# Spreading the feed's stages over its nine steps, with other shares and index loads in the tail

## The chip, the cores and the metric

One core of a Trainium2 chip runs the whole program. The metric is the device time of one execution in microseconds; lower is better. The engines are TensorE (PE, with PEld for its weight loads), VectorE (DVE), ScalarE (ACT), GpSimd (POOL) and SyncE (SP), which here issues the plain DMAs. The indirect DMAs are issued by POOL.

## What is computed

Two batches of 4096 tokens of width 256 go through a sparse attention with 16 heads of width 16, a residual sum with a layer norm, a feed part, and a second residual sum with a layer norm.

```python
scores = einsum('bhqd,bhkd->bhqk', q, k) * scale
sparsity = scores.max(axis=-1) - scores.mean(axis=-1)
_, top_idx = top_k(sparsity, U)                      # U = 307 queries of each head
out_sel = softmax(q_sel @ k.T * scale) @ v           # for the chosen queries alone
out = zeros_like(q).at[bi, hi, top_idx].set(out_sel)
x = layernorm(x + out @ Wo + bo)
xr = mu_r * x + (1 - mu_r) * x_prev ; xk = mu_k * x + (1 - mu_k) * x_prev
r = sigmoid(xr @ W_r.T) ; k = xk @ W_k.T
x = layernorm(x + r * (square(relu(k)) @ W_v.T))
```

## The kernel before

Python function `schedule()` writes one list, the plan, of tokens such as `("main", p)` or `("f2", b, t, part, bank, late)`. Every engine walks the same list and issues its own share of each token, in the order of the list. An engine is in order: what it waits for holds up everything behind it.

**The main phase** has 2048 slots, 64 for each of the 32 (batch, head) pairs. A slot is one `main` token: PE makes four 128x512 products (two into CP at L592, two into DP at L596), ACT takes the absolute value of the CP half into AB (L858), and DVE adds AB and the DP half and takes the row maximum (JK, L1014). There are two DP halves and three AB buffers. So PE can be about one slot ahead of DVE, and then waits for DVE to read a DP half (the wait on SPr in the rows).

**What rides on the slots.** After `main` a slot carries one step of the selection (`sel`, which finds the 307 queries of a group of heads), and one step of the attention over chosen queries (`att`), or, where `att` yields `None`, one step of the background (`back`). In the slots of an attention with a selection the slot behind a `cnt` or similar token, and that slot itself, carry neither (`hold`), unless bank "P" is spare. The heads are in seven groups of 8, 5, 3, 5, 5, 3 and 3.

**Attention.** For a head `hl` and a block of keys `kc` (0 to 31) `st` makes scores on PE (L688), exponentials on ACT (E, L896), and the low part of E as the difference to its bf16 high part (EL). EL is computed by POOL (L1411) for share "G" and by DVE (L1163) for share "D". `pv` follows six steps later with two products into PV (L703, L704). There are ten E buffers. At the end of a head come `fin` (ACT L903), `otr` (PE and four short DVE operations, L1170 to L1176) and `put` (POOL: L1420 and three indirect DMAs to AO, L1424). `gath` is three indirect DMAs on POOL (L1384), `arr` seven short POOL operations behind their landing.

**The feed** works through 32 tiles of 128 tokens for each batch. Tile t takes part in iterations k = t to t+9: f0 loads (SP), f1 transposes, f2 product with Wo, sum (DVE L1197) and statistics (`stats`: L1184, L1186, then `rstd` on POOL, L1430 to L1435), f3 normalises, f4 transposes, f5 mixes (POOL L1475 to L1480 in batch 0, DVE L1222 in batch 1), f6 and f6k products (tanh on ACT L934, relu on ACT L942, square on POOL L1490 in batch 0), f7 product and gating (DVE L1234, then a sum on POOL L1498 or DVE L1238), f8 statistics, f9 normalises (POOL L1511 or DVE L1251) and stores (SP L1637). `feed(0, False)` is background of the main phase. `feed(1, True)` runs alone at the end (`late`), with the f3, f5, f9 work on DVE.

**Banks.** `bank()` takes the spare PSUM banks in turn and skips the one in `state["open"]`. `attend` starts only when no bank is open. In the main phase the feed and the selection share two banks, B and P; `claim` makes PE wait until the last reader of a bank is through.

**The tail** is what follows the 2048 slots: the selection of the last group of three heads (group 6) side by side with the rest of group 5's attention, then group 6's indices, gathers and attention, then `feed(1, True)`. Background steps are taken in the tail only when no search is on.

Of the kernel before, what the change touches and what calls it, by code (L numbers as in the profile page):

```python
# [54 lines left out]
def schedule():  # L55
# [64 lines left out]
    def select(g):  # L120
# [39 lines left out]
        for h in range(n):  # L160
            yield [("idx", g, h, bank())]
        yield [("ixdma", g)]

    def prelude(g):

        n = GROUPS[g][2] if tail[0] else 1
        gaps = 0 if tail[0] else 1
        yield [("ka", 0), ("qgzero",)] if g == 0 else []
        yield [("gath", g, 0)]
        for _ in range(5 * gaps):  # L170
            yield []
        for h in range(n):
            yield [("arr", g, h)] + ([("gath", g, h + 1)] if h + 1 < n else [])
        for _ in range(4 * gaps):
            yield []
        ahead[g] = n

    def attend(g):
# [6 lines left out]
        for i in range(total + PVLAG):  # L185
            step = []
            hl, kc = divmod(i, NT)
            if i < total:
                if kc == 0:
                    step.append(("qt", g, hl, "C0"))  # L190
                    if HEAD0[g] + hl + 1 < NB * H:
                        step.append(("ka", HEAD0[g] + hl + 1))
                if kc == 10 and ahead[g] <= hl + 1 < n:
                    step.append(("gath", g, hl + 1))
                if kc == 18 and ahead[g] <= hl + 1 < n:
                    step.append(("arr", g, hl + 1))
                step.append(("st", g, hl, kc, bank(), "D" if tail[0] and kc % 2 and not state["search"] else "G"))
            j = i - PVLAG
# [3 lines left out]
            if j >= 0 and j % NT == NT - 1:  # L202
                yield [("fin", g, j // NT)]
                yield [("otr", g, j // NT, bank()), ("put", g, j // NT)]
                yield []

    def feed(b, late):
        for k in range(NT + 9):
            step = []
            for n in (9, 8, 7, 6, 5, 4, 1, 0, 3, 2):  # L210
                t = k - n
                if not 0 <= t < NT:
                    continue
                if n in (2, 6, 7):
                    for f in ("f6", "f6k") if n == 6 else ("f%d" % n,):
                        bk = state["open"] = bank()
                        for part in range(2):
                            yield step + [(f, b, t, part, bk, late)]
                            step = []
                        state["open"] = None  # L220
                elif n in (1, 4):
                    step.append(("f%d" % n, b, t, bank(), late))
                else:
                    step.append(("f%d" % n, b, t, late))
                if n == 0:
                    yield step
                    step = []
            if step:
                yield step

# [87 lines left out]
def attention_rwkv(nc, x, Wq, bq, Wk, bk, Wv, bv, Wo, bo, W_r, W_k, W_v, mu_r, mu_k, out):  # L318
    ctx = ExitStack()
    with ctx:  # L320
# [115 lines left out]
        l_w, l_z, l_m, l_i, l_q = (sem(n) for n in ("l_w", "l_z", "l_m", "l_i", "l_q"))  # L436
        l_g = [sem(f"l_g{i}") for i in range(4)]
        l_s, l_k, l_o, l_a = ([sem(f"{n}{i}") for i in range(2)] for n in ("l_s", "l_k", "l_o", "l_a"))
        l_x = [sem(f"l_x{i}") for i in range(4)]
# [515 lines left out]
        def _(dve):  # L955
# [233 lines left out]
            def f2(b, t, part, bank, late):  # L1189
# [6 lines left out]
                dve.wait_ge(f_yp, k + 1)  # L1196
                dve.tensor_tensor(fh[j], BANK[bank][:, 0:D], fx[k % 3], ALU.add).then_inc(f_y, 1)  # L1197
                dve.wait_ge(f_y, k + 1)
                stats(fh[j], j, j, f_s1, k + 1)

# [45 lines left out]
            def f9(b, t, late):  # L1246
                if late:
# [7 lines left out]
                          digit=digit, cut=cut, need=need_, rank1=rank1, rank2=rank2, slots=slots, ob=ob, oa=oa, idx=idx,  # L1255
                          st=st, otr=otr, f2=f2, f3=f3, f5=f5, f7=f7, f8=f8, f9=f9)
            for stage, *args in plan:
# [4 lines left out]
        def _(pool):  # L1262
# [110 lines left out]
            def gath(g, h):  # L1373
# [3 lines left out]
                if h == 0:  # L1377
                    pool.wait_ge(l_i, 64 * (g + 1))
                    pool.wait_ge(l_m, 32 * HEAD0[g + 1])
                if hx >= 8:  # L1380
                    pool.wait_ge(q_pool, arranged[hx - 8])
# [64 lines left out]

            def f2(b, t, part, bank, late):
                if part == 0:
                    return
                k = NT * b + t  # L1450
                after(pool, f_x1, k - 1)
                pool.wait_ge(f_s1, k + 1)
                rstd(k % 2, late).then_inc(f_r1, 1)
# [52 lines left out]
            def f9(b, t, late):  # L1506
                if not late:
# [5 lines left out]
            stages = dict(vones=vones, qzero=qzero, split=split, slots=slots, ob=ob, qgzero=qgzero, gath=gath, arr=arrange,  # L1513
                          st=st, put=put, f1=f1, f2=f2, f3=f3, f5=f5, f6k=f6k, f7=f7, f8=f8, f9=f9)
            setup()
# [5 lines left out]
        def _(sp):  # L1521
# [83 lines left out]

            def ixdma(g):
                n = GROUPS[g][2]
                sp.wait_ge(sel_ix, HEAD0[g + 1])
                sp.dma_start(IDX[g, 0:n, 0:16 * A_COLS].rearrange("h (a b) -> a h b", b=16), idw[:, 0:n, :]).then_inc(l_i, 16)
                sp.wait_ge(l_i, 64 * g + 16)  # L1610
                for c, (a0, w) in enumerate(CH):
                    sp.dma_start(idxs[g][0:w, 0:n, c], IDX[g, 0:n, a0:a0 + w].rearrange("h s -> s h")).then_inc(l_i, 16)

# [56 lines left out]
```

## Time and profile before

| | us |
|---|---|
| median of 3 runs (3490.24 to 3497.87) | 3496.7 |
| the profiled execution, whole | 3497.08 |
| its span in the profile | 3495.3 |
| busy: PE, DVE, ACT, POOL | 3113.3, 2940.5, 2878.4, 1491.0 |

The profiled execution is 1.8 us longer than its span; the rest of the text works inside the span. Stretches by the trace: the main phase ends at about 3156 us, the tail's attention and selection last until about 3330 us, and the late feed fills the rest. The feed of batch 0 lies in two stretches of the main phase, about 1990 to 2260 us and 2530 to 2790 us, with the attention of group 3 between them.

### The profile page before, as it was taken

Reading aid. Unit: us, or ns where it says so; the run is one execution under the profiler, and the core shown is the slowest. Engines: PE = TensorE matmul, PEld = TensorE weight load, DVE = VectorE, ACT = ScalarE, POOL = GpSimd, SP = SyncE. Lnnn points to the kernel's source line nnn. Section 1 sums busy time; section 2 is a strip of 40 time slices with the busy share of each in tenths; the row PEclk is TensorE's granted clock in tenths of the full one; section 3 lists DMA queues with packets and bytes.
Section 4 is the critical chain, followed back from the end, with each engine's and each line's share of the span. In section 5 each row is a group of like instructions: output and inputs, shape, how many; then the busy total and the mean of one; then the engine's idle time right before and its main releaser. Section 6 shows DMA issues by size and latency. Waiting matters only on the chain.

```text
span 3495.3 us, 58965 instructions
## 1 busy us (share of the span) xinstructions
PE 3113.3 (89%) x15985; PEld 1442.4 (41%) x15985; DVE 2940.5 (84%) x5954; ACT 2878.4 (82%) x6445; POOL 1491.0 (43%) x2634
## 2 busy tenths in 40 slices
PE   5999999998899998998999888899988898897588
PEld 3334333343244433433444444544444443344366
DVE  2889988899978888888898888888887888886478
ACT  3889888889779999899899877699976699894455
POOL 2210022100136643453556455675555653457754
PEclk8999999999989999999999999999999999997899
DMA  6432232316122241241111241121141222013022
GB/s 183 147 81 36 61 85 76 82 36 15 25 38 38 38 33 27 37 33 31 23 38 29 43 48 42 42 44 36 31 38 42 40 32 31 14 20 15 14 77 69
DMA packets 262295, 163.64 MB, mean 47 GB/s; under 512 B 167563, under 2 KB 241483, under 8 KB 257867
## 3 DMA queue, kind: packets, MB, share of 16 engines
q1 hardware_dynamic: 255819, 158.50, 24.8%
q0 software_dynamic: 6144, 1.37, 0.5%
q8 instruction: 128, 2.10, 0.3%
q14 instruction: 204, 1.67, 0.2%
HBM read 111.86 MB, written 47.86 MB: 46 GB/s over the span
## 4 chain that ended last, share of the span: by engine, by line
PE 32%; ACT 26%; issue 19%; DVE 19%; POOL 2%; DMA 1%; SPq 0%; DVEq 0%; ACTq 0%; POOLq 0%
ACT AB L858 19%; DVE JK L1014 11%; PE CP L592 10%; PE DP L596 9%; ACT E L896 4%; ACT msk L879 2%; PE PV L703 2%; PE PV L704 2%; PE BP L688 2%; DVE SPr L1014 1%; PE PV L540 1%; DVE fst L1184 1%; PE BP L726 1%; PE BP L540 1%; DVE VF L1222 1%
## 5 line engine op out<-in xcount | busy, mean ns | idle before, releaser
L1014 DVE CUSTOM_DVE_ANT_0 JK<-DP,AB 128x1024 bf16<-128x1024 f32 x2048 | 2469.0, 1222 | 384.7 <-DVE SPr L1014 137.7
L858 ACT ACTIVATE AB<-CP 128x512 f32<-128x512 f32 x4096 | 2227.3, 598 | 306.8 <-PE CP L592 253.6
L592 PE MATMUL CP<-KS,QS 128*128 128x512 f16 x4096 | 1425.3, 389 | 96.3 <-ACT AB L858 20.5
L596 PE MATMUL DP<-KS,QS 128*128 128x512 f16 x4096 | 1241.9, 385 | 70.4 <-DVE SPr L1014 63.7
L1411 POOL TENSOR_TENSOR SCR<-E 128x307 f16<-128x307 f32 x968 | 672.5, 706 | 590.7 <-ACT E L896 581.8
L592 PEld LDWEIGHTS CP<-KS,QS 128*128 128x128 f16 x4096 | 393.8, 97 | 883.7 <-ACT AB L858 762.3
L596 PEld LDWEIGHTS DP<-KS,QS 128*128 128x128 f16 x4096 | 361.6, 98 | 402.9 <-DVE SPr L1014 187.3
L896 ACT ACTIVATE E<-BP 128x307 f32<-128x307 f32 x883 | 384.5, 436 | 55.1 <-PE BP L688 53.7
L1266 POOL TENSOR_SCALAR SCR<-SCR 128x48 f16<-128x48 f16 (+2 forms) x122 | 49.6, 406 | 571.7 <-DVE SCR L982 321.6
L688 PE MATMUL BP<-QT,KA 128*128 128x307 f16 x883 | 263.1, 298 | 20.9 <-ACT QT L888 19.1
L703 PE MATMUL PV<-E,XT 128*128 128x307 bf16 x512 | 161.4, 316 | 34.2 <-POOL SCR L1411 34.0
L1014 DVE DVE_READ_ACCUMULATOR2_ANT SPr<- 128x1 f32 x2048 | 168.9, 82 | 0.0
L704 PE MATMUL PV<-SCR,XT 128*128 128x307 f16 x512 | 157.6, 308 | 0.0
L703 PE MATMUL PV<-E,VF 128*128 128x307 bf16 x512 | 153.9, 301 | 0.0
L704 PE MATMUL PV<-SCR,VF 128*128 128x307 f16 x512 | 149.7, 292 | 0.0
L688 PEld LDWEIGHTS BP<-QT,KA 128*128 128x128 f16 x883 | 87.0, 98 | 147.3 <-issue 24.2
L1384 POOL DMA_INDIRECT SCR<-QN,idxs x96 | 99.6, 1037 | 77.2 <-issue 70.4
L1424 POOL DMA_INDIRECT AO<-OG,idxs x96 | 100.8, 1050 | 34.1 <-issue 16.9
L896 ACT ACTIVATE E<-DP 128x307 f32<-128x307 f32 x115 | 47.4, 427 | 48.3 <-PE DP L688 48.1
L1430 POOL TENSOR_SCALAR frs<-fmv 128x1 f32<-128x1 f32 x128 | 29.1, 227 | 132.3 <-DVE fmv L1186 129.6
L703 PEld LDWEIGHTS PV<-E,XT 128*128 128x128 f16 x512 | 52.1, 102 | 80.4 <-POOL SCR L1411 32.7
L1431 POOL TENSOR_TENSOR frs<-frs,halfc 128x1 f32<-128x1 f32 x128 | 78.3, 612 | 10.7
(381 smaller groups left out, 2984.5 us busy)
## 6 DMA issues: line engine op xcount, KB each, us to landing
KS<-KTC SPq DMA_DIRECT2D x256, 128.0 KB, 5.0
QS<-QSC SPq DMA_DIRECT2D x512, 64.0 KB
KA<-KTC SPq DMA_DIRECT2D x128, 128.0 KB, 3.8
QN<-SCR SPq DMA_DIRECT2D x16, 544.0 KB, 3.4
SCR<-in_L_attn_x SPq DMA_DIRECT2D x16, 512.0 KB, 6.8
KTC<-SCR SPq DMA_DIRECT2D x32, 256.0 KB, 2.2
QSC<-SCR SPq DMA_DIRECT2D x32, 256.0 KB, 2.3
AO<-E SPq DMA_DIRECT2D x2, 4096.0 KB, 21.9
```

Source lines behind the costliest of these rows:

```text
L592: pe.matmul(o, qs, ks[j][:, 1, :], start=True, stop=True).then_inc(sc_c, 1)
L596: r = pe.matmul(o[:, 512 * j:512 * j + 512], qs, ks[j][:, 0, :], start=True, stop=True)
L688: pe.matmul(o[:, 0:U], KA[hx % 2][:, 128 * kc:128 * kc + 128], QT[hx % 2][:, 0:U], start=True, stop=True).then_inc(s_pe, 1)
L703: pe.matmul(PV[:, 0:U], v, EH[a % NE], start=kc == 0, stop=False)
L704: pe.matmul(PV[:, 0:U], v, EL[a % NE], start=False, stop=kc == NT - 1).then_inc(pv_pe, 1)
L858: act.activation(AB[p % 3][:, 512 * j:512 * j + 512], BANK["C%d" % j], ACT.Abs).then_inc(ab_full, 1)
L896: act.activation(E[a % NE][:], BANK[bank][:, 0:U], ACT.Exp, scale=2 * SCALE / (WS * WS)).then_inc(ex_act, 1)
L1014: dve.tensor_tensor_reduce(out=JK[p % 2][:], in0=BANK["D%d" % u], in1=AB[p % 3][:], scale=1.0, scalar=-3.0e38, op0=ALU.add, op1=ALU.max, a ...
L1384: pool.indirect_dma_start(out=QG[0:w, 3 * (hx % 8) + c, :], out_offset=None, in_=QNr[b], in_offset=bass.IndirectOffsetOnAxis(ap=ixf[0:w, k ...
L1411: pool.tensor_tensor(EL[a % NE], E[a % NE][:], EH[a % NE], ALU.subtract).then_inc(el_g, 1)
L1424: pool.indirect_dma_start(out=AOr[b], out_offset=bass.IndirectOffsetOnAxis(ap=ixf[0:w, k:k + 1], axis=0), in_=OG[i][0:w, c, :], in_offset= ...
L1431: i = pool.tensor_tensor(r[:, 0:1], r[:, 0:1], halfc[:], ALU.pow)
```

## The change

1. `feed` gives every iteration in steps of its own by a table, `products`. An entry's two halves are two steps, and stages without a product are attached to a half by name. f2's statistics become a stage of their own, `f2s`, for tile k-3. Order of an iteration before, one bracket a step: [f9 f8 f7a] [f7b] [f6a] [f6b] [f6ka] [f6kb] [f5 f4 f1 f0] [f3 f2a] [f2b with statistics]. After: [f2s f7a] [f7b] [f6a] [f8 f6b] [f6ka] [f9 f6kb] [f5 f4 f1] [f3 f2a] [f0 f2b].
2. In the first and last iterations, where a product is out of range, its attached stages are steps of their own.
3. `side` gives the share of EL. In the tail with no search on, "D" is for odd kc as before, and for all kc from 6 to 15 of a head that is not the first of its group.
4. In the tail the indices of a head are written and loaded (`ixdma`) right behind its own `idx`, with semaphores `l_t` for heads 1 and 2; `gath` of those heads waits for its own. Elsewhere one `ixdma` serves the whole group as before.

```diff
-            yield [("idx", g, h, bank())]
-        yield [("ixdma", g)]
+            yield [("idx", g, h, bank())] + ([("ixdma", g, h, h + 1)] if tail[0] else [])
+        if gaps:
+            yield [("ixdma", g, 0, n)]
...
+    def side(hl, kc):
+
+        if not tail[0] or state["search"]:
+            return "G"
+        return "D" if kc % 2 or hl and PVLAG <= kc < PVLAG + 10 else "G"
...
-                step.append(("st", g, hl, kc, bank(), "D" if tail[0] and kc % 2 and not state["search"] else "G"))
+                step.append(("st", g, hl, kc, bank(), side(hl, kc)))
...
+    def halves(k, f, n, b, late, first=(), last=()):
+
+        first, last = ([(g, b, k - m, late) for g, m in side if 0 <= k - m < NT] for side in (first, last))
+        if not 0 <= k - n < NT:
+            return [step for step in (first, last) if step]
+        bk = bank()
+        return [first + [(f, b, k - n, 0, bk, late)], last + [(f, b, k - n, 1, bk, late)]]
+
     def feed(b, late):
         for k in range(NT + 9):
...
+            products = [("f7", 7, (("f2s", 3),), ()), ("f6", 6, (), (("f8", 8),)), ("f6k", 6, (), (("f9", 9),)),
+                        None, ("f2", 2, (("f3", 3),), (("f0", 0),))]
+            for entry in products:
+                if entry is None:
+                    step = [("f5", b, k - 5, late)] if 0 <= k - 5 < NT else []
+                    for f, n in (("f4", 4), ("f1", 1)):
+                        if 0 <= k - n < NT:
+                            step.append((f, b, k - n, bank(), late))
+                    if step:
+                        yield step
                     continue
...
+                f, n, first, last = entry
+                steps = halves(k, f, n, b, late, first, last)
+                for step in steps:
+                    held = [token[4] for token in step if token[0] == f]
+                    if held:
+                        state["open"] = held[0]
                     yield step
...
+                state["open"] = None
...
+            def f2s(b, t, late):
+                k = NT * b + t
                 dve.wait_ge(f_y, k + 1)
-                stats(fh[j], j, j, f_s1, k + 1)
+                stats(fh[k % 2], k % 2, k % 2, f_s1, k + 1)
...
+                if h and g + 1 == len(GROUPS):
+                    pool.wait_ge(l_t[h - 1], 64)
...
+            def ixdma(g, h0, h1):
+                l = l_i if h0 == 0 else l_t[h0 - 1]
+                base = l_seen.get(l, 0)
+                sp.wait_ge(sel_ix, HEAD0[g] + h1)
+                sp.dma_start(IDX[g, h0:h1, 0:16 * A_COLS].rearrange("h (a b) -> a h b", b=16),
+                             idw[:, h0:h1, :]).then_inc(l, 16)
+                sp.wait_ge(l, base + 16)
```

## Rows read from the trace of the kernel before

**Rows 1.** Windows: length, busy time of each engine, clock, DMA share, GB/s.
```profile
1990.00:2260.00 270.00, 232.63 (x1252) 125.13 (x1251) 221.82 (x503) 193.28 (x464) 159.30 (x380) 0.96 0.24 40
...
3156.00:3262.00 106.00, 62.18 (x485) 38.05 (x485) 50.06 (x226) 34.62 (x84) 79.75 (x142) 0.73 0.30 16
3262.00:3334.00 72.00, 47.13 (x309) 30.98 (x309) 36.80 (x64) 40.59 (x102) 52.46 (x65) 0.86 0.08 17
3334.00:3495.20 161.20, 139.06 (x768) 113.11 (x768) 140.39 (x416) 95.05 (x320) 78.18 (x160) 0.96 0.25 77
```

**Rows 2.** The same windows for L1014 alone, two instructions a slot.
```profile
1990.00:2260.00 270.00, 176.10 (x288) 0.96 0.24 40
2262.00:2520.00 258.00, 227.08 (x371) 1.00 0.21 40
```

**Rows 3.** Waits, 1990 to 2260 us: total, times, longest.
```profile
POOL VF L1490 <- ACT VF L942: 58.6, 13, 8.0
...
PEld DP L596 <- DVE SPr L1014: 27.4, 39, 1.7
DVE JK L1014 <- ACT AB L858: 24.8, 20, 2.1
```

**Rows 4.** Timeline, start and length, DVE in one feed iteration.
```profile
2106.67 0.41 DVE L1197 TENSOR_TENSOR VF<-BP,VF 128x256 f32<-128x256 f32 x1
2107.11 0.43 DVE L1184 BATCH_NORM_STATS2 fst<-VF 128x6 f32<-128x256 f32 x1
...
2107.72 1.23 DVE L1014 CUSTOM_DVE_ANT_0 JK<-DP,AB 128x1024 bf16<-128x1024 f32 x1
...
2110.62 0.42 DVE L1234 SCALAR_TENSOR_TENSOR VF<-VF,BP 128x256 f32<-128x256 f32 x1
```

**Rows 5.** Timeline of PE, a stall behind DVE in the first feed stretch.
```profile
2059.53 0.70 PE L726 MATMUL BP<-W_rT,VF 128*128 128x256 f32 x2 [1.89 <-DVE W_k L1234]
```

**Rows 6.** Groups by line, POOL, 1990 to 2260 us: count, busy, mean ns, idle before.
```profile
L1431 POOL TENSOR_TENSOR frs<-frs,halfc 128x1 f32<-128x1 f32 x31 | 17.6, 568 | 2.6
...
L1511 POOL TENSOR_SCALAR VF<-VF,frs 128x256 f32<-128x256 f32 x6 | 3.3, 550 | 0.0
```

**Rows 7.** Timeline of the tail, from group 6's first indices to its last `arr`.
```profile
3224.00 0.16 DVE L1155 SCALAR_TENSOR_TENSOR idw<-CP,hoff 20x16 int32<-20x16 f32 x1 [6.70 <-PE CP L667]
...
3228.95 0.29 SPq L1609 DMA_DIRECT2D IDX<-idw  x1
...
3233.23 1.16 POOL L1384 DMA_INDIRECT SCR<-QN,idxs  x1 [1.33 <-DMA idxs<-IDX]
...
3238.77 0.54 POOL L1266 TENSOR_SCALAR SCR<-SCR 128x48 f16<-128x48 f32 x2 [1.46 <-DMA SCR<-QN,idxs]
...
3244.44 0.71 POOL L1411 TENSOR_TENSOR SCR<-E 128x307 f16<-128x307 f32 x1
...
3255.10 2.67 POOL L1411 TENSOR_TENSOR SCR<-E 128x307 f16<-128x307 f32 x4
```

**Rows 8.** Timeline of the tail, group 6's first head and what follows it.
```profile
3274.13 1.62 ACT L896 ACTIVATE E<-DP 128x307 f32<-128x307 f32 x4
...
3274.26 8.70 DVE L1163 TENSOR_TENSOR SCR<-E 128x307 f16<-128x307 f32 x10 [0.32 <-ACT E L896]
...
3287.17 1.02 POOL L1424 DMA_INDIRECT AO<-OG,idxs  x1 [0.40 <-POOL OG L1420]
...
3287.61 0.48 DVE L1163 TENSOR_TENSOR SCR<-E 128x307 f16<-128x307 f32 x1 [0.32 <-ACT E L896]
...
3291.12 4.54 POOL L1411 TENSOR_TENSOR SCR<-E 128x307 f16<-128x307 f32 x6
3291.88 0.31 PE L703 MATMUL PV<-E,XT 128*128 128x307 bf16 x1 [3.71 <-POOL SCR L1411]
...
3294.29 0.46 PE L688 MATMUL DP<-QT,KA 128*128 128x307 f16 x1
...
3295.06 0.47 PE L688 MATMUL DP<-QT,KA 128*128 128x307 f16 x1
```

More of the change, by code:

```diff
@@ L205, in attend @@
                 yield []
+    def halves(k, f, n, b, late, first=(), last=()):
[4 more added lines that the diff above has]
+        return [first + [(f, b, k - n, 0, bk, late)], last + [(f, b, k - n, 1, bk, late)]]
     def feed(b, late):
         for k in range(NT + 9):
[L209 to L212, printed above, removed]
-                    continue
[L214 to L225, printed above, removed]
+            products = [("f7", 7, (("f2s", 3),), ()), ("f6", 6, (), (("f8", 8),)), ("f6k", 6, (), (("f9", 9),)),
[8 more added lines that the diff above has]
+                        yield step
+                    continue
+                f, n, first, last = entry
[4 more added lines that the diff above has]
+                        state["open"] = held[0]
                     yield step
-                    step = []
-            if step:
-                yield step
+                state["open"] = None
     def background():
@@ L437, in attention_rwkv @@
         l_g = [sem(f"l_g{i}") for i in range(4)]
+        l_t = [sem(f"l_t{i}") for i in range(GROUPS[-1][2] - 1)]
         l_s, l_k, l_o, l_a = ([sem(f"{n}{i}") for i in range(2)] for n in ("l_s", "l_k", "l_o", "l_a"))
@@ L1255, in _ @@
                           digit=digit, cut=cut, need=need_, rank1=rank1, rank2=rank2, slots=slots, ob=ob, oa=oa, idx=idx,
-                          st=st, otr=otr, f2=f2, f3=f3, f5=f5, f7=f7, f8=f8, f9=f9)
+                          st=st, otr=otr, f2=f2, f2s=f2s, f3=f3, f5=f5, f7=f7, f8=f8, f9=f9)
             for stage, *args in plan:
@@ L1445, in f1, with f2s @@
                 pool.tensor_tensor(fx[k % 3], fx[k % 3], bob[:], ALU.add).then_inc(f_xb, 1)
-            def f2(b, t, part, bank, late):
-                if part == 0:
-                    return
+            def f2s(b, t, late):
                 k = NT * b + t
@@ L1513, in _ @@
             stages = dict(vones=vones, qzero=qzero, split=split, slots=slots, ob=ob, qgzero=qgzero, gath=gath, arr=arrange,
-                          st=st, put=put, f1=f1, f2=f2, f3=f3, f5=f5, f6k=f6k, f7=f7, f8=f8, f9=f9)
+                          st=st, put=put, f1=f1, f2s=f2s, f3=f3, f5=f5, f6k=f6k, f7=f7, f8=f8, f9=f9)
             setup()
@@ L1604, in sel @@
                                  SB[g][:, u, h, :].unsqueeze(2)).then_inc(l_m, 16)
[L1606 to L1610, printed above, removed]
+            def ixdma(g, h0, h1):
[5 more added lines that the diff above has]
+                sp.wait_ge(l, base + 16)
                 for c, (a0, w) in enumerate(CH):
-                    sp.dma_start(idxs[g][0:w, 0:n, c], IDX[g, 0:n, a0:a0 + w].rearrange("h s -> s h")).then_inc(l_i, 16)
+                    sp.dma_start(idxs[g][0:w, h0:h1, c], IDX[g, h0:h1, a0:a0 + w].rearrange("h s -> s h")).then_inc(l, 16)
+                l_seen[l] = base + 64
+            l_seen = {}
             def ka(hx):
```

## The prediction

> **What bounds the kernel now.** I read the page's busy times first (the table above): PE, DVE and ACT all have over 80% of the span, so no engine alone sets the time, and I went by stretches. In the windows [rows 1] the reader is to see three regimes that the change touches. In the first feed stretch no engine is full (DVE 221.82 of 270 us, PE 232.63), and the slots are slow: 288 instructions are 144 slots, 270 / 144 = 1.875 us each, against 258 / 185.5 = 1.39 us in the attention between the feed stretches [rows 2]. In the tail DVE, PE and ACT have much idle and POOL is the busiest (79.75 of 106 us, 52.46 of 72). In the late feed DVE has 140.39 of 161.2 us, its filling and draining included. The waits then say what the feed stretch loses: PE's weight loads stand 27.4 us in 39 waits for DVE to read a DP half, while DVE elsewhere stands 24.8 us for ACT's AB [rows 3]. Each is late in turn: that is what a clump does, and what a fuller DVE would not show.
>
> **Part 1, the main feed spread.** The timeline of DVE [rows 4] shows the clump: sum at 2106.67, statistics of the sum until the JK at 2107.72, then, each behind another JK, the statistics of f8 and the gating at 2110.62. Statistics cost 2107.72 - 2107.11 = 0.6 us, the sum 0.44, the gating 0.35 (its neighbour starts before it ends). So three slots in a row get 1.05 + 0.6 + 0.35 = 2.0 us of feed on DVE, and six get none. After, they get 0.44, 0.6 and 0.35 = 1.4 us, and 0.6 more comes two slots later with f8. No work vanishes. Gained is what PE loses to DVE being late, at most 0.6 us a tile, on 32 tiles 19 us. It is less, for three reasons. Where the search's many small DVE operations fill DVE (the one-hot compares of `ob` and `oa`) DVE bounds whatever the order. Most waits on a DP half are short (27.4 / 39 = 0.7 us), not all after the clump. And f8 meets a DVE that has had one slot to catch up. For it speaks the second kind of stall: f6 takes the bank that f7 left, and stands 1.89 us for the gating [rows 5]; such I find five in this stretch, each at most 0.6 us shorter after. I take 4 us less stall on DP halves in both stretches (out of 2 x 27.4, the second stretch's own being smaller) and 3 us for the bank stalls (ten by 0.3): **-7 us**, bounds 0 and -16. Below nothing: the reorder moves POOL's f9 ahead of the square, see the rivals.
>
> What else moves hides. f0 is two slots later, but is used nine slots on. SP's f9 store waits for POOL's f9 five slots later than before, and what is queued on SP behind it (the next head's keys and queries) is asked for tens of slots ahead. POOL's `rstd` of f2s waits for DVE's statistics one step later; behind it stands the f7 sum, needed by f8 an iteration on. POOL waits 58.6 / 13 = 4.5 us for relu before a square [rows 3], and f9 (0.55 us [rows 6]) falls into that.
>
> **Part 2, the number of steps.** Counted from the code, the feed had 293 steps and gets 304: in iterations 3 to 6 and 32 to 40 attached stages stand alone. From its first slot, 1325, to 1487 it has 163 slots. Before, the 163rd step closed a bank. After, it is f7's second half, the bank is open, `attend` waits until slot 1493, five slots late. Group 3's attention then ends in slots with group 4's search, where `hold` costs it four more. The second stretch begins at slot 1682 and not 1673, and at 1803 step 290 is reached. One more step closes the bank. So group 4 starts one slot late, and thirteen steps are left for which the main phase has no empty slot: f7 of tile 30, f6, f6k and f7 of tile 31, f8 of 29 to 31, f9 of 28 to 31. They go where the tail next takes background: right when group 6's search ends.
>
> For the main phase this is about one tile less. Nine slots at the difference of the two rates, 9 x (1.875 - 1.39), give **-4 us** (bounds 0 and -6; search and attention rates differ too).
>
> **Part 3, the indices head by head, and the thirteen steps.** Before, POOL's queue is the chain here [rows 7]: all indices out at 3228.95, first gather at 3233.23, `arr` and the next gather 3238.77 to 3244.44 = 5.7 us, and so on, until POOL comes back to EL at 3255.10. After, head 0's indices can leave 3228.95 - 3224.00, nearly 5 us, earlier [rows 7], but POOL has first to do the EL of the block queued ahead of the gather, whose scores PE makes behind the third `idx`. I place the gather near 3230.3: -2.9 us. The two further index loads are done long before their gathers. Then come the thirteen steps. On POOL: three `rstd` at about 1.2 us (0.57 of it L1431), four f9 at 0.55 [rows 6], two f7 sums and a square at 0.6 to 0.65: 3.6 + 2.2 + 1.9 = 7.7 us. Two of them, 1.9 us, fall into the waits for the gathers' landing (1.46 us each [rows 7]). Against that stands a new wait: PE's f7 of tile 31 waits for POOL's square, which is queued behind the last `arr`, so the attention products behind it wait too, then POOL waits about 1.6 us for PE and DVE to return the gating. 7.7 - 1.9 + 1.6 - 2.9 = **+4.5 us**. Bounds: -2.9, if all hides under POOL's landings and DVE's share of EL (blocks up to 15 no longer need POOL), and +8 if nothing does.
>
> **Part 4, the other shares.** Between heads of group 6 POOL is in `put` from 3287.17 to 3291.12, and the EL of even blocks are queued behind it; PE stands 3.71 us [rows 8]. Afterwards PE is on its lower level, 1.2 GHz (the stretch's mean granted clock is 0.86 [rows 1]): scores are 0.77 us apart at 3294.29 and 3295.06, against 1.62 / 4 = 0.40 us in full flow, four such intervals, 1.5 us. After the change DVE makes blocks 6 to 15. Alone it takes 0.48 us a block, and it does so during POOL's `put` [rows 8]; PE and ACT go 0.40 us a step. Six steps of lag cover the difference (10 x 0.08 = 0.8 us). POOL is back for block 16 at 3291.1, wanted at about 3292. Two transitions at 3.7, one of them with the 1.5: **-8.9 us**. Bounds -1 and -10. The stall before group 6's first head stays (head 0 is excluded).
>
> Here a page speaks against the change. The Trainium skill, SBUF — State Buffer, section Who interferes with whom, says that a DVE instruction with two SBUF inputs contends with a GpSimd instruction that reads SBUF, and that the loser is blocked for the whole of it. The trace agrees for pairs of EL: DVE's ten take 8.70 us beside POOL's ten [rows 8], not ten times 0.48. It doesn't show it for `put`: the DVE block at 3287.61 is 0.48 us long inside POOL's 1.02 us. By the row the sum is the -8.9 above; by the page, with `put` holding DVE off, it would be rival D.
>
> **Part 5, the late feed.** DVE's cyclic order there was sum, f2 statistics, f9, f8, f7, f5, f3. It becomes sum, f2s, f7, f8, f9, f5, f3: the same instructions, and no idle between them to win. f9's store and the f0 loads behind it on SP go out about 1.4 us later, with 2.65 us to land, before the transposes of the next iteration 4.5 us on: just hidden, and another 1.3 us until DVE would wait. In the last iterations DVE used to do f8 and f9 while waiting for f7's product, and now does them behind it: 0.6 us of statistics and 0.3 of f9, less 0.3 as the very last f9 no longer stands ahead: **+0.6 us**.
>
> **Sum.** -7 - 4 + 4.5 - 8.9 + 0.6 = -14.8. The profiled execution took 3497.08 us (span 3495.3, and 1.8 around it): 3482.3. The median is 0.4 us below it, nothing against the rest: I say **3482 us**.
>
> **Rivals.** The forecast as summed, 3476 to 3487 of its own, has chance 0.42.
> B: spreading gives nothing, since DVE from the sum to f8 has the same total, and stays late over all five slots. For it: DVE's 82% and the small operations. Against: 24.8 us in which DVE waits for AB. -4 - 3.8 = -7.8: 3489. Chance 0.22.
> C: the thirteen steps hide in the tail, as PE, DVE and ACT are idle there most of the time. For it [rows 1]; against it that POOL isn't. -7 - 4 - 2.9 - 8.9 + 0.6 = -22.2: 3475. Chance 0.18.
> D: in the tail `put` blocks DVE's EL, and the stall only changes its owner; 1 us is left of the 8.9. -7 - 4 + 4.5 - 1 + 0.6 = -6.9: 3490. Chance 0.08, by the one row against it.
> E, slower: POOL comes late with f5 in the main feed. Its queue gets f9 and the `rstd` of f8 between f7's sum and the square, and f6 of the next iteration waits for f5. It decides once POOL's 4.5 us in front of the square is used up: each further half microsecond costs 32 x 0.5 = 16 us, with no gain from part 1: 3489.3 + 16 = 3505. Against: the moved operations are 1.8 us, not 4.5. Chance 0.10.
>
> **The numbers.** What measurement can tell from no change is about 0.2%, 7 us. Faster: the forecast, C, half of B, some of D: 0.74. Same: the rest of B and D: 0.16. Slower: E, 0.10. The range from 3470 to 3494 holds the forecast and B to D, 0.90 together, less a tenth for the outer ends of their own bounds (spreading worth twice the 7, the thirteen steps at +8); E is left out.
>
> **What would show it.** Waits of PE on SPr in the feed stretches down from 27.4 us, and below 1.875 us a slot. Behind the last `arr` POOL lines of f9 and `rstd` among the EL, and PE waiting for L1490's successor. No 3.71 us wait of PV between heads of group 6, and ten DVE EL in a row. The forecast fails if spreading gives none or twice of what I take, or if the thirteen steps land elsewhere.

## The result and the profile after

| | before | after |
|---|---|---|
| median (lowest to highest), us | 3495.88 (3490.24 to 3497.87), 4 runs | 3471.08 (3469.15 to 3476.23), 4 runs |
| ratio | | 0.9934 [0.9917, 0.9951] |
| profiled execution, its span | 3497.08, 3495.3 | 3471.34, 3469.6 |

The change is faster by 24.8 us by the medians and by 23.1 us by the ratio; the ratio's interval reaches from 17 to 29 us. Forecast were 14.8 us less and 3482 us, in a range from 3470 to 3494; the time lies in it, near its lower end.

The page of the changed kernel: busy times, and two groups of instructions (count, busy, mean ns, idle before and what ended most of it). The JK line is now L1028, the product into DP L610.

```profile
PE 3101.0 (89%) x15985; PEld 1435.5 (41%) x15985; DVE 2950.1 (85%) x5969; ACT 2875.2 (83%) x6445; POOL 1481.5 (43%) x2619
...
L1028 DVE CUSTOM_DVE_ANT_0 JK<-DP,AB 128x1024 bf16<-128x1024 f32 x2048 | 2467.9, 1222 | 364.9 <-DVE SPr L1028 129.2
...
L610 PEld LDWEIGHTS DP<-KS,QS 128*128 128x128 f16 x4096 | 361.3, 98 | 385.0 <-DVE SPr L1028 169.7
```

The work is the same and the busy times with it; what shrank is idle time. The windows that answer to [rows 1] (busy PE, PEld, DVE, ACT, POOL, then clock, DMA share, GB/s):

```profile
1990.00:2260.00 270.00, 233.34 (x1286) 125.50 (x1285) 230.82 (x523) 200.43 (x479) 162.69 (x384) 0.99 0.29 46
...
3136.00:3240.00 104.00, 63.88 (x485) 39.16 (x485) 53.13 (x231) 35.37 (x87) 81.92 (x149) 0.70 0.29 17
3240.00:3307.00 67.00, 46.44 (x324) 30.01 (x322) 42.17 (x76) 40.20 (x105) 46.81 (x57) 0.90 0.12 25
3307.00:3469.60 162.60, 139.08 (x768) 113.19 (x767) 141.55 (x416) 95.05 (x320) 78.68 (x160) 0.95 0.25 76
```

In the same 270 us of the feed DVE did 230.82 us of work and not 221.82, and the clock stood at 0.99 and not 0.96. L1028 alone in the windows of [rows 2], and then from slot 1325 to 1488, to 1673, to 1808 and to the last slot. The bounds are the starts of the slots' JK; the last three numbers are again clock, DMA share and GB/s:

```profile
1990.00:2260.00 270.00, 184.28 (x304) 0.99 0.29 46
2262.00:2520.00 258.00, 228.71 (x373) 1.00 0.19 35
...
1977.46:2272.82 295.36, 198.61 (x328) 0.98 0.29 47
2272.82:2529.68 256.86, 226.71 (x371) 1.00 0.21 36
2529.68:2774.19 244.51, 164.25 (x270) 0.98 0.24 40
2774.19:3133.42 359.23, 291.51 (x478) 0.98 0.18 24
```

The same four stretches of the kernel before:

```profile
1980.38:2285.95 305.57, 199.16 (x328) 0.96 0.27 48
2285.95:2542.80 256.85, 226.70 (x370) 1.00 0.21 35
2542.80:2798.69 255.89, 165.06 (x270) 0.95 0.25 38
2798.69:3154.36 355.67, 291.44 (x479) 0.99 0.17 24
```

304 instructions are 152 slots, 270 / 152 = 1.78 us each against 1.875 before. The two stretches with the feed are 10.2 and 11.4 us shorter, the one between them is the same to 0.01 us, and 3.6 us are given back after slot 1808. The slots are the same and what rides on them isn't quite: by the plan the feed now has slots 1325 to 1483 and 1667 to 1807, where it had 1325 to 1487 and 1673 to 1802. So of the 25.7 us between the spans, 1155.96 - 1173.98 = -18.0 belong to the main phase from slot 1325 on, -4.8 to what follows the last slot (3495.3 - 3154.36 = 340.9, now 3469.6 - 3133.42 = 336.2), and -2.9 to the slots ahead of 1325, where the plan is the same in both. That last part is chance; what it is made of comes below.

The waits that answer to [rows 3], the same window:

```profile
POOL frs L1449 <- DVE fmv L1200: 81.6, 28, 8.7
...
DVE JK L1028 <- ACT AB L872: 23.9, 23, 2.1
PEld DP L610 <- DVE SPr L1028: 21.4, 37, 1.8
...
DVE JK L1028 <- PE DP L610: 2.7, 2, 2.2
```

PE's wait for a DP half went from 27.4 to 21.4 us, and POOL's slack moved from before the square to before the `rstd`, where it costs nothing. Of rival E's late POOL little came: from slot 1325 to 1488 PE's feed products stood 2.8 us for POOL in two waits, before in none, and from slot 1667 to 1808 3.4 us, before 4.1.

### The profile page after: what moved, and what is told of

It reads as the page before. It is cut to its first block, busy times and chain, and to the rows that moved or that the text cites. A ratio compares the mean times of both kernels' runs of the same rounds, so it can differ in the third digit from the quotient of the medians.

```text
span 3469.6 us, 58976 instructions
## 1 busy us (share of the span) xinstructions
PE 3101.0 (89%) x15985; PEld 1435.5 (41%) x15985; DVE 2950.1 (85%) x5969; ACT 2875.2 (83%) x6445; POOL 1481.5 (43%) x2619
## 4 chain that ended last, share of the span: by engine, by line
PE 30%; ACT 28%; issue 19%; DVE 19%; POOL 2%; DMA 1%; SPq 0%; ACTq 0%; DVEq 0%; POOLq 0%
ACT AB L872 21%; DVE JK L1028 11%; PE CP L606 10%; PE DP L610 8%; ACT E L910 4%; ACT msk L893 2%; PE PV L717 2%; PE PV L718 2%; PE BP L702 1%; DVE VF L1239 1%; DVE fst L1198 1%; PE PV L554 1%; DVE SPr L1028 1%; PE BP L554 1%; PE BP L740 1%
## 5 line engine op out<-in xcount | busy, mean ns | idle before, releaser
L1028 DVE CUSTOM_DVE_ANT_0 JK<-DP,AB 128x1024 bf16<-128x1024 f32 x2048 | 2467.9, 1222 | 364.9 <-DVE SPr L1028 129.2
L610 PE MATMUL DP<-KS,QS 128*128 128x512 f16 x4096 | 1238.5, 384 | 60.7 <-DVE SPr L1028 54.2
L1430 POOL TENSOR_TENSOR SCR<-E 128x307 f16<-128x307 f32 x953 | 661.0, 706 | 583.8 <-ACT E L910 574.6
L610 PEld LDWEIGHTS DP<-KS,QS 128*128 128x128 f16 x4096 | 361.3, 98 | 385.0 <-DVE SPr L1028 169.7
L1028 DVE DVE_READ_ACCUMULATOR2_ANT SPr<- 128x1 f32 x2048 | 169.8, 83 | 0.0
L717 PEld LDWEIGHTS PV<-E,XT 128*128 128x128 f16 x512 | 52.0, 101 | 76.5 <-POOL SCR L1430 27.2
```

What stands on the lines that cost most here:

```text
L610: r = pe.matmul(o[:, 512 * j:512 * j + 512], qs, ks[j][:, 0, :], start=True, stop=True)
L717: pe.matmul(PV[:, 0:U], v, EH[a % NE], start=kc == 0, stop=False)
L1028: dve.tensor_tensor_reduce(out=JK[p % 2][:], in0=BANK["D%d" % u], in1=AB[p % 3][:], scale=1.0, scalar=-3.0e38, op0=ALU.add, op1=ALU.max, a ...
L1430: pool.tensor_tensor(EL[a % NE], E[a % NE][:], EH[a % NE], ALU.subtract).then_inc(el_g, 1)
```

## The experiments

All kernels were timed against the kernel before on their own chip; e1 to e4 share a chip, so do e5 to e8, and e9 to e11. The stretches are read from one profiled execution each, as above: slots 0 to 1325 (no feed in them, the same plan in every kernel), the two feed stretches, all of slot 1325 to the last, and from the last slot to the end of the span.

| kernel | ratio [95%] | 0 to 1325 | 1325 to 1488 | 1673 to 1808 | 1325 to last | last to end |
|---|---|---|---|---|---|---|
| before | | 1897.1 | 305.6 | 255.9 | 1174.0 | 340.9 |
| the change | 0.9934 [0.9917, 0.9951] | 1894.3 | 295.4 | 244.5 | 1156.0 | 336.2 |
| e1 new feed alone | 0.9957 [0.9942, 0.9973] | 1894.1 | 295.0 | 244.8 | 1153.8 | 344.7 |
| e2 tail alone | 0.9976 [0.9964, 0.9988] | 1902.9 | 307.5 | 255.2 | 1175.6 | 331.2 |
| e3 statistics moved | 1.0007 [0.9996, 1.0017] | 1892.3 | 307.8 | 256.1 | 1177.0 | 340.4 |
| e4 304 steps, old order | 0.9982 [0.997, 0.9994] | 1890.6 | 303.8 | 247.3 | 1167.3 | 347.3 |
| e5 e4 and f8 moved | 0.9973 [0.9961, 0.9984] | 1899.7 | 299.6 | 243.4 | 1161.3 | 350.7 |
| e6 new order, 294 steps | 0.9969 [0.9957, 0.9981] | 1901.3 | 303.8 | 249.5 | 1166.5 | 342.5 |
| e7 change, one index load | 0.9939 [0.992, 0.9958] | 1891.4 | 295.3 | 244.5 | 1153.4 | 336.8 |
| e8 294 steps, best tail | 0.9918 [0.9899, 0.9936] | 1901.0 | 300.1 | 247.8 | 1160.1 | 326.6 |
| e9 change, best tail | 0.9915 [0.9901, 0.9929] | 1900.8 | 296.1 | 244.8 | 1156.2 | 326.3 |
| e10 e4, f8 and statistics moved | 0.9958 [0.9945, 0.997] | 1900.4 | 294.1 | 241.3 | 1149.7 | 350.7 |
| e11 the change again | 0.9926 [0.9913, 0.9939] | 1900.7 | 295.8 | 244.6 | 1154.0 | 333.7 |

**e1, the new feed alone**, with the old shares and one index load; **e2, the tail's two edits alone**, with the old feed.

```diff
 e1:
-        return "D" if kc % 2 or hl and PVLAG <= kc < PVLAG + 10 else "G"
+        return "D" if kc % 2 else "G"
-            yield [("idx", g, h, bank())] + ([("ixdma", g, h, h + 1)] if tail[0] else [])
-        if gaps:
-            yield [("ixdma", g, 0, n)]
+            yield [("idx", g, h, bank())]
+        yield [("ixdma", g, 0, n)]
 e2: feed() as before, f2's statistics as a token f2s in the step of f2's second half
```

Expected of e1:

> The new feed alone; the tail's shares of EL and the one index load are as before. The full change took 20.9 us off the main phase (last JK 3154.3 to 3133.4 us) and 4.7 off what follows. Theory S (the order inside an iteration is what counts in the main phase): about -19 us of the kernel's 3496, the last JK near 3135 us, and a tail some 7 us longer than with the full change. Theory N (half of the main phase's gain is alignment or chance of that execution, the spread itself is worth my forecast of 7): last JK near 3145 us, time near 3487.

Expected of e2:

> The other shares and the indices head by head alone; the feed as before. From the trace of the full change I expect the two transitions in group 6 to give 7.5 us, and the head-by-head indices about 3 us now that no feed step follows them: -10 us, 3486. If the main phase were helped by the tail parts in any way (it should not be, their tokens come after it), the last JK would move from 3154; I expect it within 3 us. Rival (the index loads bring nothing, as POOL's queue only waits elsewhere): -7.5 us, 3488.

e1 took 0.43% off (15 us, its interval 9 to 20), between its two theories; e2 0.24% (8.4 us), between its own two. Together 23.4 us, which is what the change gives (0.66%, 23.1): within the intervals the two halves don't touch each other. The feed carries nearly two thirds, where the forecast had only 7 + 4 - 7.4 - 0.6 = 3.0 us of its 14.8 there.

**e3, only the statistics of the sum a step later**, and **e4, only the number of steps**.

```diff
 e3, in feed(), before the loop over n:
+            if 0 <= k - 3 < NT:
+                step.append(("f2s", b, k - 3, late))
 e4, in feed():
         for k in range(NT + 9):
+            if 3 <= k <= 6:
+                yield []
...
+            for _ in range({1: 1, 32: 1, 33: 1, 34: 1, 38: 2, 39: 1}.get(k, 0)):
+                yield []
```

Expected of e3:

> The feed in the old order of stages and steps, but the statistics of f2 taken out of its second half and put first in the next iteration (f2s, f9, f8, f7a in one step); tail as before. DVE's clump is then 0.44, 1.2, 0.35 us in three slots in place of 1.05, 0.6, 0.35: the same sum. Theory S by clump size over three slots: no gain, within 2 us. Rival (the single slot counts, 1.2 instead of 1.05 us): 2 to 4 us slower. Rival (the statistics are in the way of the JK that PE waits for just when it also waits for the sum): 3 to 8 us faster.

Expected of e4:

> The old order of stages, with eleven empty steps at the places where the new feed has steps of its own in its first and last iterations: 304 steps, so group 3's attention starts at slot 1484 and not 1488, group 4's at 1808, and bank turns fall as in the new feed. Theory S: nothing but the steps moved into the tail, -2 to +2 us. Rival A (alignment of the attention's start and of the banks' turns made part of the 20.9 us): -5 to -10 us, last JK below 3149 us.

e3 is no change at all: the statistics of the sum then fall into the slot of f8's statistics, the gating comes behind both, and three slots in a row still hold 0.44, 1.2 and 0.35 us. e4 is 0.18% faster with nothing spread. The rows say where; L1025 is its JK line:

```profile
1975.36:2279.16 303.80, 199.22 (x328) 0.96 0.31 47
...
2537.53:2784.78 247.25, 164.82 (x271) 0.97 0.22 40
```

Of its 6.7 us in the main phase 8.6 come in the second feed stretch and 1.8 in the first, and 3.7 are given back elsewhere. Its tail took 6.4 us more (clock 0.84 and not 0.86). So from slot 1325 to the end its profiled execution took 1514.7 us against 1514.9, no gain; the 6.3 us by the ratio, with an interval from 2 to 10, are all that speaks for one. In the plan, group 5's attention starts at slot 2034 and not 2030, so four of its steps move from the main phase into the tail, beside three leftover stages of the feed. From the last search to the PV copy of group 5's last head the four kernels with 304 steps and the old tail (e1, e4, e5, e10) took 59.8 to 60.5 us, those with 293 or 294 (before, e3, e6) 57.5 to 58.2. Group 6's three heads took 64.6 to 64.8 us there and 62.5 to 62.6 here; why these are slower no run shows.

**e5, f8 moved on top of e4** (in the old order, to the second half of f6), and **e10, both DVE moves on top of e4**, with f9, f0 and f1 left where they were.

```diff
 e5, against e4:
-            for n in (9, 8, 7, 6, 5, 4, 1, 0, 3, 2):
+            for n in (9, 7, 6, 5, 4, 1, 0, 3, 2):
...
+                            if (f, part) == ("f6", 1) and 0 <= k - 8 < NT:
+                                step = step + [("f8", b, k - 8, late)]
...
-            for _ in range({1: 1, 32: 1, 33: 1, 34: 1, 38: 2, 39: 1}.get(k, 0)):
+            for _ in range({1: 1, 32: 1, 33: 1, 34: 1, 38: 1, 39: 1}.get(k, 0)):
 e10, against e5:
+            if 0 <= k - 3 < NT:
+                step.append(("f2s", b, k - 3, late))
...
-    yield step + [(f, b, t, part, bk, late)] + ([("f2s", b, t, late)] if (n, part) == (2, 1) else [])
+    yield step + [(f, b, t, part, bk, late)]
```

Expected of e5:

> As the run with the eleven empty steps, but the statistics of f8 are moved from the iteration's first step to the one with f6's second half; f2's statistics stay with its sum, f9 and f0 stay. In that run slots 1325 to 2047 took 1167.3 us, in the full change 1155.9. Theory S (DVE's clump over three slots, 2.0 us, is what costs; f8 is the only stage that leaves it): near 1156 to 1158 us, the whole gain of order. Rival (f2's statistics and f8's both have to move): 1162 to 1166 us.

Expected of e10:

> The old order with 304 steps (as in the run with empty steps) and with both DVE moves of the change: the statistics of the sum one step later, f8 in f6's second half; f9, f0, f1 and the rest stay where they were; old tail. Theory 1 (the gain of the order is the clump on DVE, and it goes only when both of its statistics have moved, which is why moving one alone gave 0 and about 3 us): 0.9955, within 1 us of the new feed alone, about 3483. Theory 2 (the gain of the order on top of the count needs f9 and f0 moved too, that is POOL's and SP's queues): no more than the run with f8 alone, 0.9973 or above, 3489.

e5's 1161.3 us fell between the two forecasts, nearer to that of the rival (0.9973 against e4's 0.9982, intervals overlapping). e10 stands at 0.9958 beside the new feed's 0.9957:

```profile
1984.96:2279.06 294.10, 198.55 (x329) 0.98 0.31 48
...
2535.98:2777.30 241.32, 164.25 (x271) 0.99 0.23 41
```

One move alone gives 0 (e3, on the old count of steps), the other about 3 us, both give 0.24% = 8.4 us over e4, and the moves of f9 and f0 add nothing that shows: from slot 1325 to the end e10 took 1500.4 us and e1 1498.5. So the gain of the order comes from the two moves on DVE. Before, there are 1.05, 0.6 and 0.35 us of small operations in three slots; e3 has 0.44, 1.2, 0.35, e5 1.05, 0, 0.35, and only e10 and the change have no slot with more than one of them, 0.44, 0.6, 0.35. Theory S of e5, that the sum over three slots is what costs, is not borne out: e5's sum is 1.4 us as in the change, and it has 3 of the 8.4 us. The largest amount in one slot doesn't order the runs alone either, since e5 and before both have 1.05. That the clump is the reason is argued from the order; shown is that it takes both moves. The tail of both is 3 to 4 us longer than e4's, nearly all in the late feed, from the last head's PV copy to the last store: e4 166.2 us, e5 and e10 169.3, the new feed 168.0, before 166.9. There f8 behind the product costs about 3 us, of which moving f9 as well gives 1.3 back.

**e6, the new order in 294 steps**: the edge stages are carried into the next step, so that the attentions start at 1488 and 1804 and nothing is left to the tail; old tail.

```diff
                     if step:
-                        yield step
+                    if k in (1, 32, 33, 34):
+                        carry = carry + step
+                    elif carry + step:
+                        yield carry + step
+                        carry = []
...
+                    if len(steps) == 1 and (3 <= k <= 6 and f == "f7" or k in (38, 39) and f == "f6"):
+                        carry = step
+                        continue
```

Expected:

> The new order inside the iterations, but the stages that stood alone at the edges are joined to their neighbours, so that the feed has 294 steps, attention starts at slots 1488 and 1804 as before, and no feed step is left for the tail; tail otherwise as before. Theory S: the order alone gives what it gives on top of the step count, 11 to 13 us in slots 1325 to 2047 (1174.0 before, so about 1162), and the tail keeps its 336.7 us plus 1.7 for the late feed. Time about -10 us, 3486 to 3488. Rival (the order only works together with the shifted attention and bank turns): above 1170 us, no gain.

0.9969: the order without the number of steps is worth 10.8 us by the ratios, the number without the order 6.3 (e4), and both 15.0 (e1); each of the three is uncertain by some 4 us or more. In the main phase e6's profiled execution gained 7.5 us, and e8's, whose main phase is the same program, 13.8. The first feed stretch of the two, e6 and then e8:

```profile
1985.84:2289.59 303.75, 198.69 (x328) 0.96 0.34 45
```

```profile
1984.34:2284.44 300.10, 198.66 (x328) 0.97 0.34 46
```

3.65 us apart with the same instructions, and the clock with it. One execution tells an order's worth to no better than that.

**e7, the change with one index load for group 6.**

```diff
-            yield [("idx", g, h, bank())] + ([("ixdma", g, h, h + 1)] if tail[0] else [])
-        if gaps:
-            yield [("ixdma", g, 0, n)]
+            yield [("idx", g, h, bank())]
+        yield [("ixdma", g, 0, n)]
```

Expected:

> The full change with one index load for group 6 as before. With both, the stretch from the cut of group 6's search to the end of group 5's last head took 58.3 us; with neither, 59.8. If the head-by-head loads give what POOL's first gather showed (2.9 us earlier after the cut), this run takes 60 to 61 us there and is 2 us slower than the full change, 3473. Rival (nothing, since POOL's queue absorbs it): the same as the full change within 1 us.

0.9939 against 0.9934 and 0.9926: the times can't tell it. The trace can: from the last search to the PV copy of group 5's last head it took 60.0 us, where the change took 58.3 and 57.0. So the index loads head by head are worth 1.7 to 3.0 us in that stretch, as forecast.

**e8 and e9, versions to beat both.** Both keep the old order in the late feed and give DVE blocks 0 to 9 of group 6's first head too. e8 has the main feed of e6, e9 that of the change. **e11** is the change itself beside e9.

```diff
-        return "D" if kc % 2 or hl and PVLAG <= kc < PVLAG + 10 else "G"
+        return "D" if kc % 2 or (PVLAG if hl else 0) <= kc < PVLAG + 10 - (0 if hl else PVLAG) else "G"
...
-    for step in feed(1, True):
+    for step in feed_late(1, True):
```

Expected of e8:

> The full change with three things mended that its trace shows: the 294-step feed, so that no feed step lies in the tail (2.4 us in front of group 5's last head by comparison, and none of the waits on POOL behind the gathers), the late feed in its old order (1.7 us), and DVE's share for blocks 0 to 9 of group 6's first head, which stands 4.3 us behind POOL's stores. Expected against before: -18 to -12 in the main phase (less if the shifted attention is worth 6.7 us by itself), -15 to -17 after it: -28 to -33 us, 3465 to 3470, so 3 to 8 us below the full change. Rival (bank turns and the attention's start are worth more than the tail's steps cost): above 3471, no better than the full change.

Expected of e9:

> The change, with two parts of it made otherwise: the late feed in its old order (the new one cost about 1.5 us), and DVE's full share for blocks 0 to 9 of group 6's first head too. Against the run that had both of these with the 294-step feed (0.9918): if the count of steps is worth 4 to 6 us in the main phase and 2.4 us of it come back in the tail, this one is at 0.990 to 0.991, 3464 to 3467. If the count is worth nothing: 0.9918 to 0.9925, 3470 to 3473.

Expected of e11:

> The changed kernel itself, on the chip of the two others, so that they can be set against it. 0.9934, 3475.

e9 is at 0.9915 [0.9901, 0.9929] and 3467.88 us, the change beside it at 0.9926 [0.9913, 0.9939] and 3474.27 us. By the medians it is 6.4 us ahead and by the ratios 3.8; the intervals overlap, so that it is better is likely and not shown by the times alone. It fell between its two forecasts. In the trace the tail is where it should be: 326.3 us from the last slot on, against 336.2 and 333.7. Group 6's first head in e9, timeline of PE, DVE and POOL (L726 makes the scores, L1201 is EL on DVE, L1467 `put`):

```profile
3249.54 0.72 PE L726 MATMUL DP<-QT,KA 128*128 128x307 f16 x4 [0.65 <-ACT QT L926]
...
3250.46 4.21 DVE L1201 TENSOR_TENSOR SCR<-E 128x307 f16<-128x307 f32 x10 [1.12 <-ACT E L934]
...
3250.13 1.09 POOL L1467 DMA_INDIRECT AO<-OG,idxs  x1 [0.43 <-POOL OG L1463]
```

DVE makes the ten blocks while POOL is in `put`, PE has no wait for an EL behind it, and the head takes 18.5 us from PV copy to PV copy (3247.65 to 3266.19) where the change takes 22.9. e8 missed its forecast: 3473.0 us where 3465 to 3470 were expected, and its rival had said above 3471. By the ratio, 0.9918, it is still ahead of the change (0.9934, and e7's 0.9939 on e8's own chip), intervals overlapping. Whether 294 or 304 steps is better under this tail stays open, since e8 and e9 ran on different chips.

## Why the prediction was right, and where it wasn't

The direction and the range held, and so did the mechanism of the shares (part 4). Spreading was right as a cause and too small as a term, and the count of steps was wrong in its reason. The sum was 8 to 10 us short (23.1 by the ratio and 24.8 by the medians against 14.8). Term by term:

**Part 1, spreading: -7 forecast, about -9 to -13 found.** With the number of steps held at 304, the main phase from slot 1325 took 1167.3 us in the old order (e4) and in five executions of the new one 1156.0, 1153.8, 1153.4, 1156.2 and 1154.0, mean 1154.7: -12.6, with e4 read from one execution. The ratios say -8.7 (e1 against e4), the late feed's loss in it. This is the term that was mis-sized most. Of its two pieces the one on DP halves was right: in slots 1325 to 1488 and 1673 to 1808 PE's weight loads stood 54.3 us for a DP half before, 48.1 in e4 and 44.3 after, so the order has 3.8 of it, 4 forecast. The other, -3 us on bank stalls, is not there: in the first feed stretch the waits of PE's feed products (L726, now L740) for DVE add up to 10.5 us, as before, with their longest at 1.8 instead of 1.9. And one piece was missing from the sum: the clock.

The stall of [rows 5] is an example. PE in the kernel before, busy time and clock, then two products into DP on either side:

```profile
2057.00:2059.00 2.00, 0.60 (x2) 1.00 0.09 32
2059.00:2061.00 2.00, 1.47 (x7) 0.99 0.72 39
2061.00:2064.40 3.40, 3.40 (x12) 0.50 0.68 68
```

```profile
2060.50 0.60 PE L596 MATMUL DP<-KS,QS 128*128 128x512 f16 x2
...
2062.60 1.06 PE L596 MATMUL DP<-KS,QS 128*128 128x512 f16 x2
```

PE stands for the gating, 1.89 us, and a little later the granted clock is at 0.50, 1.2 GHz, and a pair of 128x512 products takes 1.06 us and not 0.60. A mean clock of 0.96 over 305.6 us and of 0.95 over 255.9 is 24 + 26 = 50 us at the lower level; after, 0.98 in both stretches is 12 + 10 = 22 us. What such time costs is read where the plan is the same. Slots 511 to 643 of the changed kernel, and of e7, which has the same plan there:

```profile
778.32:985.33 207.01, 158.58 (x264) 0.93 0.37 29
```

```profile
779.65:980.93 201.28, 158.47 (x264) 0.98 0.47 29
```

29 us at the lower level against 8, and 5.7 us of time: 0.27 us for each. The 28 us that the change saves in the feed stretches are then about 7.6 us; e4, with 24 + 15 = 39 us at the lower level, has 11 of the 28, the order the other 17, which is 4.6 us. That is an estimate, since the rate is from slots without the feed, and in the feed the stalls in front of a fall cost time themselves. With it the order comes to -4 - 4.6 = -8.6, what the ratios say; the 4 us more in the traces I can't assign. Not every pause is followed by a fall. Before, each of the twelve falls of the clock in the two feed stretches comes shortly behind a pause of PE, the shortest of them 1.19 us. But the pause of 1.92 us at 2139.5 us has none behind it, and one of 2.88 us had a fall behind it before (at 2067.1 us) and none after (at 2067.0). So a part of the clock's share can be chance. The Trainium skill, TensorE: Matmul & The Clock Gate, section Terms, counts half of the time at the lower level as lost. The rows say 0.27 of it here, where DVE and ACT limit the slots as much as PE does.

**Part 2, the number of steps: in the main phase the size was near, the reason wrong.** This is the step that failed: "`attend` waits until slot 1493, five slots late", the second stretch "begins at slot 1682 and not 1673", and "thirteen steps are left". In the plan as it is made, group 3's attention starts at 1484, four slots earlier than before. I had taken 1488 for the first slot in which it could start. It could at 1484, and in the old plan it only waited there for f6's and f6k's bank; with the shifted steps none is open then. The second stretch ends at 1808 and four short steps are left to the tail, f9 of tiles 29, 30 and 31 and f8 of 31. The extra steps are there, but by themselves they are nothing to do: a feed of 304 steps does less in each slot. In e4 the main phase gained 6.7 us against 4 forecast, and its tail lost 6.4, where I had put nothing but the leftover steps. Since the attentions start four slots late from group 4 on, four steps of group 5's attention are left to the tail too, which the forecast doesn't have. So how much the count is worth in all stays open: nothing by e4's trace, 2 to 10 us by its ratio.

**Part 3: +4.5 forecast, about +1 found.** The tail of the changed kernel, which answers to [rows 7] (L1528 is f9, L1430 EL):

```profile
3202.92 0.16 DVE L1169 SCALAR_TENSOR_TENSOR idw<-DP,hoff 20x16 int32<-20x16 f32 x1 [2.07 <-PE DP L681]
3203.11 0.28 SPq L1627 DMA_DIRECT2D IDX<-idw  x1
...
3210.29 1.12 POOL L1403 DMA_INDIRECT SCR<-QN,idxs  x1 [0.17 <-issue]
...
3222.26 0.55 POOL L1528 TENSOR_SCALAR W_k<-W_k,frs 128x256 f32<-128x256 f32 x1
...
3229.83 0.56 POOL L1528 TENSOR_SCALAR W_k<-W_k,frs 128x256 f32<-128x256 f32 x1
...
3232.96 2.67 POOL L1430 TENSOR_TENSOR SCR<-E 128x307 f16<-128x307 f32 x4
3233.72 0.44 PE L717 MATMUL PV<-E,XT 128*128 128x307 bf16 x1 [19.30 <-POOL SCR L1430]
```

The index load leaves right behind the head's own `idw`. From `idw` to the first gather it is 7.4 us, before 9.2; from the first gather to EL 22.7 us, before 21.9, with one `rstd` and two of the leftover f9 in between, the latter in the time in which POOL would wait for the gathers to land. From the last slot to the PV copy of group 5's last head it took 108.5 us and, in e11, 107.9, against 107.2 before. With thirteen steps I had 7.4 us for the leftovers; the four cost at most 2.4 (the change against e2, from the last search to that copy, 58.3 and 55.9), since the four attention steps of group 5 that came into the tail with them are in this figure. The -2.9 of the index loads was right (e7).

**Part 4: -8.9 forecast, -7.7 and -9.5 found.** From the PV copy of group 5's last head to that of group 6's second, before 3261.51 to 3324.12 = 62.6 us are now 3241.88 to 3296.76 = 54.9, and 53.2 in e11. e2, which has the old feed and so differs here by the shares alone, took 54.0: -8.6. In e1, with the new feed and the old shares, the stretch took 64.8, so beside the new feed the shares give 10 to 12 us, and the new count of steps takes 2 back. The transition that answers to [rows 8]:

```profile
3266.48 4.13 DVE L1177 TENSOR_TENSOR SCR<-E 128x307 f16<-128x307 f32 x10
...
3267.39 1.02 POOL L1443 DMA_INDIRECT AO<-OG,idxs  x1 [0.28 <-POOL OG L1439]
3268.71 1.18 POOL L1443 DMA_INDIRECT AO<-OG,idxs  x1 [0.30 <-issue]
3270.19 1.37 POOL L1443 DMA_INDIRECT AO<-OG,idxs  x1 [0.30 <-issue]
...
3271.58 3.62 POOL L1430 TENSOR_TENSOR SCR<-E 128x307 f16<-128x307 f32 x5
...
3272.58 4.12 DVE L1177 TENSOR_TENSOR SCR<-E 128x307 f16<-128x307 f32 x4 [0.55 <-ACT E L910]
...
3272.64 0.31 PE L717 MATMUL PV<-E,XT 128*128 128x307 bf16 x1 [0.43 <-POOL SCR L1430]
...
3275.60 0.31 PE L717 MATMUL PV<-E,XT 128*128 128x307 bf16 x1 [1.60 <-DVE SCR L1177]
```

The 3.71 us of PE are 0.43 here; 1.60 come back a little later, when DVE and POOL are again making blocks side by side (four in 4.12 us), and the score products stay at 0.40 us a step. Rival D is out: ten blocks take 4.13 us, 0.41 each, across three indirect DMAs of POOL. The Trainium skill, SBUF — State Buffer, section Who interferes with whom, leaves room for that: it infers that `tensor_tensor` takes only the read interface of the shared pair and that making descriptors needs the write interface. The trace agrees. Pairs of EL, where both engines read SBUF, still hold each other up: nine on either engine take 7.83 and 7.81 us in e9, 0.87 a pair. But the loser isn't blocked for the whole of the other's instruction, as the prediction took it: alone they take 0.48 us on DVE and 0.71 on POOL, which would be 1.19 a pair.

**Part 5: +0.6 forecast, +1.7 found** (166.9 to 168.6 us from the last PV copy to the last store; 168.3 in e11), most of it f8's new place (e5).

**The rivals.** B, that spreading gives nothing, is out as a whole, and yet moving one of the two statistics gave nothing (e3). C's time, 3475, is the nearest to the result, for another reason: the leftover steps were few rather than hidden. E never came near. The forecast of 3482 us has some luck in it: its own bounds, 3476 to 3487, missed the 3471.08, and the range held it by the room that was left for C. The two terms of the feed were short by 8 us together and the thirteen steps were too dear by 3.5, both in the same direction.

The found terms add up to -12.6 - 6.7 + 1 - 8.6 + 1.7 = -25.2, against 24.8 by the medians and 22.8 and 27.2 in the two traces of the change once the slots ahead of 1325 are left out. These are stretches of time laid end to end, so that they add up proves nothing of their causes: work that moved from the main phase to the tail is a gain in the second term and a loss in the third and fourth.

## What to carry to other kernels

Small operations that ride on a loop can cost by how they are clumped and not by their sum alone, and the clump has to be broken up whole: moving one of the two gave 0 or 3 us, moving both gave 8. A pause of PE may have to be priced twice, once as the pause and once as the slower clock that can follow it, at a rate read from two executions of the same stretch. When an edit changes how many steps a schedule has, print the plan and read the slots from it; the count by hand was wrong in its sign, and put thirteen steps in the tail where four came. Where a stretch gets shorter, look in the plan for work that left it: four steps of attention did here.

## What the runs showed of the hardware

Executions of the same stretch differ mostly by the clock. In the 13 profiled executions slots 0 to 1325 have the same plan, and took from 1890.6 us (e4) to 1902.9 us (e2), with between 26 and 70 us of them at 1.2 GHz; the two go together with a correlation of 0.97, at 0.26 us for each microsecond at the lower level. That spread, 12 us, is half of what the change gives, in one profiled execution against another. It is why the stretches of a plan were compared here, and not the spans.
